# Last attention of an eight-sublayer network: the next layer's rows are normed by GpSimd, turned in other PSUM banks, and the router's products start inside the last unit

## The chip, the cores and the metric

The program runs on one core of one Trainium2 chip. The metric is the device time of one execution in microseconds (us), from the runs of the kernel. The core has five engines: TensorE (PE, matrix products and transposes, writes PSUM), VectorE (DVE), ScalarE (ACT), GpSimd (POOL, cannot read PSUM) and SyncE (SP, here the queue that issues the transfers). Each works through its own list of instructions in order and waits on semaphores for the others.

## The reference, cut to what matters

The network has four pairs of a cross-attention and a feed-forward part, each with a residual sum and a layer norm ahead of it. The change touches only the last pair. `x` is (8, 256, 512), the context (8, 256, 256).

```python
x = x + _L3_xattn_ref(_layernorm(x), ctx_1024, Wq, Wk, Wv, Wo, gq, gk)
x = x + _L3_ffn_ref(_layernorm(x), router_w, router_b, expert_w, expert_b)

def _layernorm(x, eps=1e-05):
    return (x - mean(x)) / sqrt(var(x) + eps)

def _L3_xattn_ref(h, c, Wq, Wk, Wv, Wo, gq, gk):       # 16 heads of 128
    q, k = rmsnorm(h @ Wq, gq), rmsnorm(c @ Wk, gk)    # per head
    attn = softmax(q k^T / sqrt(128))
    return (attn @ (c @ Wv)) @ Wo

def _L3_ffn_ref(x, router_w, router_b, expert_w, expert_b):   # 16 experts
    S = softmax(x.reshape(2048, 512) @ router_w + router_b)
    G, idx = top_k(S.T, 128)                                  # 128 tokens per expert
    ...                                                       # G * (tokens @ expert_w + expert_b), added back
```

## The kernel before

The residual stream `X` lies in SBUF as 16 tiles of 128 tokens by 512. A layer norm of tile t is: DVE takes the statistics (`dve_stat`: `st`, `mv`) and adds the epsilon (`sc`, L94); GpSimd raises it to -1/2 (`rsqrt`, L220, writes `rs`); DVE makes the normed rows `xn` (L95, two buffers, t mod 2); PE turns them with four 128x128 transposes into one PSUM bank (`pe_ln`, L218, banks 0 and 1 by t mod 2); ACT copies the bank to the high part `XH` (L84); DVE writes the low part `XL` = bank - `XH` (L90). Each product of the network is then three products of high and low parts.

The last attention is `wide_steps(3)`: 64 units, unit u for head pair u // 8 and batch u % 8, software-pipelined. All engines walk the same list of steps, and each issues its share of a step. The steps of unit u in order (letters of `order`):

- Q, `proj` u+1: PE makes the keys (bank 1), the queries (bank 0) and the values (bank 2). ACT squares the keys, DVE sums them (`kst`), GpSimd raises them (`kst`), DVE scales them to `K1` and writes `QL`, `VL`.
- 0, `out` (u-1, 0): PE multiplies the attention output by Wo (six products, bank 7), DVE adds the bank to the residual tile (`X<-X,banks`).
- T, `turn` u: PE turns the normalised probabilities `P` in banks 4 and 5, ACT and DVE split them into `PH`, `PL`.
- L, `late` u+1: PE turns `K1` in bank 1 and sums the squared queries with a column of ones; ACT and DVE write `KH`, `KL`; DVE writes `qst`, GpSimd raises it; `ctx` u+2: ACT and GpSimd split the context into `CH`, `CL`.
- 1, `out` (u-1, 1); S, `scores` u+1 (banks 2, 3; DVE maxima `mx`, `nb`; ACT exponentials `P`, L81); P, `pv` u (bank 6); N, `norm` u+1 (DVE `rc`, `P`); E, `pvout` u (`OH`, `OL`).

In the last eight units each `out` (v, i), v >= 56, completes a residual tile t = 2(v - 56) + i. Right behind it DVE takes the statistics of tile t and then does the whole norm step of tile t - 1 (`dve_ln`: `sc` of the next, `xn` of tile t, which waits for GpSimd's `rs`, and `XL` of tile t - 1); PE turns tile t - 1 right behind the `out` products (L827 and on), in bank 0 or 1, and so waits there:

```python
                if not l0 and (t := 2 * (v - 56) + i - 1) >= 0:
                    if v + 2 >= 64:
                        pe.wait_ge(S["kl3"], 64)
                        pe.wait_ge(S["qst"], 64)
                    elif t % 2:
                        pe.wait_ge(S["kst"], 3 * v + 9)
                    else:
                        pe.wait_ge(S["qst"], v + 3)
                    self.pe_ln(pe, 7, t)
```

Because bank 0 also holds the queries and bank 1 the keys, the following K turn and `proj` steps wait for `XL` of that tile (`wait_xt(pe, 7, ...)`). Behind the 64 units come three groups of router products (`pe_choice_logits` 0 to 2: 12 products of 16x512 each, banks 4 and 5), a fence of all engines, the turn of tile 15, router products 3, and 16 turns of the logits (`cWK`). From there the choice of tokens and the expert products run on; the change does not touch them.

Two steps `choice` (in units 58 and 59) put the split of the expert weights (`cwh` on ACT, `cwl` on DVE) behind those units.

Of the kernel before, what the change touches and what calls it, by code (L numbers as in the profile page):

```python
# [159 lines left out]
class Program:  # L160
# [184 lines left out]
    def act_ln(self, act, n, t):  # L345
# [10 lines left out]
        act.acopy((self.XH if n in LN_SPLIT else self.XF)[:, :, tok], src).then_inc(S["xh"], 1)  # L356

    def wait_xt(self, e, n, t):
# [8 lines left out]
    def wide_steps(self, L):  # L367
        l0 = L == 0

        if l0:  # L370
            yield "fetch", 0
            for t in range(4):
                yield "ln", t
            yield "part", 0
        yield "fetch", 1
        yield "proj", 0
        if not l0:
            yield "late", 0
            yield "ctx", 1
        yield "scores", 0  # L380
        yield "norm", 0
        side = 0
        for u in range(64):
            for step in "Q0TL1SPNE" if not l0 else "QT0SP1NE":
                if l0 and u >= 1 and step in "T0N" and side < NSIDE:
                    yield "side", side
                    side += 1
                if step == "Q" and u + 1 < 64:
                    if (u + 1) % 8 == 0:
                        yield "fetch", (u + 1) // 8 + 1  # L390
                    if (u + 1) % 8 == 5:
                        yield "part", (u + 1) // 8 + 1
                    yield "proj", u + 1
                    if not l0 and (u + 1) % 8 == 7:
                        yield "partkv", (u + 1) // 8 + 1
                if step == "T":
                    yield "turn", u
                if step == "L" and u + 1 < 64:
                    yield "late", u + 1
                    if u + 2 < 64:  # L400
                        yield "ctx", u + 2
                if step == "S" and u + 1 < 64:
                    yield "scores", u + 1
                if step == "0":
                    if u + 2 < NB:
                        yield "ln", 2 * u + 4
                        yield "ln", 2 * u + 5
                    if u >= 1:
                        yield "out", (u - 1, 0)
                if step == "1" and u >= 1:  # L410
                    yield "out", (u - 1, 1)
                if step == "P":
                    yield "pv", u
                if step == "E":
                    yield "pvout", u
                if step == "N" and u + 1 < 64:
                    yield "norm", u + 1
            if not l0 and u in (56, 58, 59):
                yield "choice", u
        yield "out", (63, 0)  # L420
        yield "out", (63, 1)

# [226 lines left out]
    def pool_wide(self, pool, L):  # L649
        S, w, l0 = self.S, self.W[L], L == 0  # L650
        n = 0 if l0 else 6
        for step, u in self.wide_steps(L):
# [11 lines left out]
            if not l0 and step == "late":  # L664
                pool.wait_ge(S["qst"], u + 1)
                pool.wait_ge(S["exp"], 4 * (64 + u))
                self.rsqrt(pool, w["qst"][:, 1, :], w["qst"][:, 0, :]).then_inc(S["qrs"], 1)
            if not l0 and step == "out" and (t := 2 * (u[0] - 56) + u[1] - 1) >= 0:
                self.pool_ln(pool, 7, t)

# [5 lines left out]
    def pe_wide(self, pe, L):  # L676
# [5 lines left out]
        for step, u in self.wide_steps(L):  # L682
# [11 lines left out]
            if step == "proj":  # L694
# [29 lines left out]
                if not l0:  # L724
                    pe.wait_ge(S["qst"], u)
                    if u >= 59:
                        self.wait_xt(pe, 7, 2 * u - 118)
                for h in range(2):
# [13 lines left out]
            if step == "late":  # L742
                k, z = banks[1], banks[0]
                pe.wait_ge(S["kst"], 3 * u + 3)
                if u < 7:
                    self.wait_xt(pe, n, min(2 * u + 3, NT - 1) if u else 3)
                if u >= 59:
                    self.wait_xt(pe, 7, 2 * u - 117)
                for i in range(2):
# [8 lines left out]
            if step == "turn":  # L758
                for qt in range(2):
                    z = banks[4 + qt]  # L760
                    pe.wait_ge(S["pl"], 2 * U - 1 + qt)
                    pe.wait_ge(S["n"], self.wide_n(L, u, 6))
                    for kt in range(2):
# [49 lines left out]
            if step == "out":  # L813
# [12 lines left out]
                pe.mms(z[:], terms).then_inc(S["y"], 1)  # L826
                if not l0 and (t := 2 * (v - 56) + i - 1) >= 0:  # L827
                    if v + 2 >= 64:
                        pe.wait_ge(S["kl3"], 64)
                        pe.wait_ge(S["qst"], 64)  # L830
                    elif t % 2:
                        pe.wait_ge(S["kst"], 3 * v + 9)
                    else:
                        pe.wait_ge(S["qst"], v + 3)
                    self.pe_ln(pe, 7, t)

    def act_wide(self, act, L):
# [9 lines left out]
        for step, u in self.wide_steps(L):  # L847
# [68 lines left out]
            if step == "out" and not l0 and (t := 2 * (u[0] - 56) + u[1] - 1) >= 0:  # L916
                self.act_ln(act, 7, t)

# [8 lines left out]
    def dve_wide(self, dve, L):  # L927
# [9 lines left out]
        for step, u in self.wide_steps(L):  # L937
# [11 lines left out]
            if step == "proj":  # L949
# [7 lines left out]
                else:  # L957
# [59 lines left out]
            if step == "out":  # L1017
# [2094 lines left out]
    def act_choice_logits(self, act, k):  # L3112
        S, w = self.S, self.W["c"]
        act.wait_ge(S["lz"], k + 5)
        act.acopy(w["WK"][:, 512 * k:512 * k + 512], self.banks[4 + k % 2][0:16, :]).then_inc(S["lg"], 1)

# [33 lines left out]
    def pe_choice(self, pe):  # L3150
        S, w, banks = self.S, self.W["c"], self.banks
        self.pe_ln(pe, 7, NT - 1)
        self.pe_choice_logits(pe, 3)
# [45 lines left out]
    def act_choice(self, act):  # L3199
        S, w, banks = self.S, self.W["c"], self.banks  # L3200
        self.act_ln(act, 7, NT - 1)
        self.act_choice_logits(act, 3)
# [24 lines left out]
    def dve_choice(self, dve):  # L3227
# [12 lines left out]

        self.dve_ln(dve, 7, NT - 1)
        dve.red(w["E16"][:], self.ident[:].rearrange("p (t e) -> p e t", t=8), ALU.add).then_inc(S["ctop"], 1)
# [106 lines left out]
    def pe_program(self, e):  # L3349
# [22 lines left out]
    def act_program(self, e):  # L3372
# [16 lines left out]
        self.act_wide(act, 3)  # L3389
        for k in range(3):  # L3390
            self.act_choice_logits(act, k)
        self.fence(act, 7)
# [142 lines left out]
```

## Time and profile before

| | us |
|---|---|
| median of 3 runs (3707.21 to 3717.07) | 3714.59 |
| the profiled execution, device time | 3713.18 |
| its span, first to last instruction | 3711.4 |
| PE busy | 3375.3 (91%) |
| DVE busy | 2365.6 (64%) |
| ACT busy | 1578.8 (43%) |
| POOL busy | 1255.7 (34%) |
| mean granted TensorE clock | 0.959 |

All positions below are microseconds from the start of the span. The last attention ends near 3640; the units before 3489 each take about 13.4 us. A busy share of a whole span is an average over unlike stages, so the stretch from 3462 to 3645 is read by itself: by windows that begin where DVE adds the first half of a unit's output to `X`, by DVE's waits, and by single rows of the timeline.

### The profile page before, as it was taken

The numbers are of one execution on the slowest core, as the hardware profiler recorded it, in microseconds if no ns is written. First come the engines' busy times: TensorE is split into PE (matmuls) and PEld (weight loads), VectorE is DVE, ScalarE is ACT, GpSimd is POOL, SyncE is SP. The second block draws the span as 40 slices with busy tenths as digits, with TensorE's granted clock in tenths as the row PEclk, the third lists the DMA queues.
The fourth block names the chain that finished last, engine by engine and source line by source line (L and its number), as shares of the span: only waits on it lengthen the run. The fifth ranks groups of instructions, "written<-read, shape, count | busy, mean of one in ns | idle before, by whom it ended". The sixth has DMA issues, their size and how long they took to land.

```text
span 3711.4 us, 60483 instructions
## 1 busy us (share of the span) xinstructions
PE 3375.3 (91%) x22678; PEld 2749.8 (74%) x22678; DVE 2365.6 (64%) x4653; ACT 1578.8 (43%) x3417; POOL 1255.7 (34%) x1168
## 2 busy tenths in 40 slices
PE   7999999959999689988999889997889999999977
PEld 6899998937778456656998644443789999999865
DVE  6677777863323478866444467774677777777766
ACT  5666665531111255542222233343245555555531
POOL 1013334111243477732222345554422222222212
PEclk9999999978999899999999889998999999999989
DMA  3246665124645110001111154542000000000001
GB/s 131 80 135 224 231 224 181 37 86 164 242 172 191 69 28 28 11 5 69 35 35 38 30 139 113 128 116 50 27 7 18 13 18 18 18 7 18 13 1 48
DMA packets 153784, 296.92 MB, mean 80 GB/s; under 512 B 18040, under 2 KB 71416, under 8 KB 148760
## 3 DMA queue, kind: packets, MB, share of 16 engines
q1 hardware_dynamic: 147256, 272.60, 23.1%
q0 software_dynamic: 6240, 20.45, 1.6%
q8 instruction: 184, 3.01, 0.3%
q14 instruction: 104, 0.85, 0.1%
HBM read 390.12 MB, written 95.68 MB: 131 GB/s over the span
## 4 chain that ended last, share of the span: by engine, by line
PE 37%; DVE 8%; issue 3%; POOL 2%; ACT 1%; DMA 1%; SPq 0%; POOLq 0%; DVEq 0%; ACTq 0%
PE banks L107 34%; PE banks L218 3%; DVE nrec L2656 1%; DVE nmx L101 1%; ACT P L81 1%; DVE xn L95 0%; POOL kst L90 0%; DVE X L90 0%; DMA nqT<-nmT 0%; DVE st L274 0%; DVE PL L90 0%; DVE X L98 0%; POOL rs L90 0%; DVE KL L98 0%; DVE P L94 0%
## 5 line engine op out<-in xcount | busy, mean ns | idle before, releaser
L90 DVE TENSOR_TENSOR X<-X,banks 128x512 f32<-128x512 f32 x352 | 239.9, 683 | 192.5 <-PE banks L107 192.2
L101 DVE TENSOR_REDUCE nmx<-banks 128x4 f32<-128x1024 f32 (+2 forms) x256 | 238.8, 954 | 122.3 <-PE banks L107 122.2
L81 ACT ACTIVATE nPT<-banks 128x1024 f32<-128x1024 f32 x192 | 196.4, 1023 | 239.8 <-PE banks L107 239.6
L107 PE MATMUL banks<-XH,wqh 128*128 128x256 f32 x1024 | 292.3, 285 | 0.0
L107 PE MATMUL banks<-XL,wqh 128*128 128x256 f32 x1024 | 286.7, 280 | 0.0
L107 PE MATMUL banks<-XH,wql 128*128 128x256 f32 x1024 | 286.4, 280 | 0.0
L107 PE MATMUL banks<-XH,tT 128*128 128x256 f32 x1024 | 246.3, 284 | 8.3 <-DVE XL L90 5.4
L90 POOL TENSOR_TENSOR slo<-sraw,shi 128x512 fp32r<-128x512 f32 x96 | 126.0, 1313 | 374.7 <-ACT shi L84 374.7
L107 PE MATMUL banks<-XL,tT 128*128 128x256 f32 x1024 | 245.1, 283 | 0.0
L107 PE MATMUL banks<-woh,OH 128*128 128x512 f32 x512 | 219.3, 428 | 12.2 <-DVE OL L90 10.3
L81 ACT ACTIVATE P<-banks,nb,qst 128x256 f32<-128x256 f32 x256 | 141.2, 561 | 190.7 <-DVE nb L90 190.7
L107 PE MATMUL banks<-WU,exh 128*128 (+1 forms) x624 | 207.5, 404 | 14.3 <-DMA WU<-expert_parts 12.7
L107 PE MATMUL banks<-woh,OL 128*128 128x512 f32 x512 | 206.6, 404 | 0.0
L107 PE MATMUL banks<-wol,OH 128*128 128x512 f32 x512 | 206.5, 403 | 0.0
L107 PEld LDWEIGHTS banks<-XH,tT 128*128 128x128 f32 x1024 | 196.7, 192 | 11.1 <-DVE XL L90 7.1
L90 POOL TENSOR_TENSOR nPS<-nPT 128x512 f32<-128x512 f32 x128 | 162.6, 1271 | 114.7 <-PE banks L107 95.9
L107 PEld LDWEIGHTS banks<-XL,tT 128*128 128x128 f32 x1024 | 196.7, 192 | 0.8
L107 PEld LDWEIGHTS banks<-XH,wqh 128*128 128x128 f32 x1024 | 195.8, 191 | 0.0
L107 PEld LDWEIGHTS banks<-XL,wqh 128*128 128x128 f32 x1024 | 193.8, 189 | 0.0
L107 PEld LDWEIGHTS banks<-XH,wql 128*128 128x128 f32 x1024 | 193.5, 189 | 0.0
L90 POOL TENSOR_TENSOR kst<-kst,mhalf 128x4 f32<-128x4 f32 x64 | 64.6, 1009 | 364.7 <-DVE kst L95 364.7
L90 DVE TENSOR_TENSOR PL<-banks,PH 128x512 fp32r<-128x512 f32 x256 | 164.6, 684 | 29.9 <-ACT PH L84 29.0
(443 smaller groups left out, 10122.6 us busy)
## 6 DMA issues: line engine op xcount, KB each, us to landing
WU<-expert_parts SPq DMA_DIRECT2D x39, 4096.0 KB
WD<-expert_parts SPq DMA_DIRECT2D x39, 2048.0 KB
sraw<-in_moe_w SPq DMA_DIRECT2D x96, 256.0 KB, 3.3
expert_parts<-shi SPq DMA_DIRECT2D x96, 256.0 KB
expert_parts<-slo SPq DMA_DIRECT2D x96, 256.0 KB
head_stacks<-nTK SPq DMA_DIRECT2D x48, 256.0 KB
head_stacks<-nTQ SPq DMA_DIRECT2D x48, 256.0 KB, 3.0
nkT<-head_stacks SPq DMA_DIRECT2D x64, 192.0 KB, 4.5
```

What stands on the lines that cost most here:

```text
L81: return self.e.activation(out, in_, func, **kw)
L90: return self.e.tensor_tensor(out, a, b, op)
L101: return self.e.tensor_reduce(out, a, AX.X, op, **kw)
L107: return self.e.matmul(out, l, r, start=start, stop=stop, skip_group_check=skip)
L218: return pe.e.transpose(out, in_, self.ident[0:n, 0:n])
L2656: dve.e.reciprocal(w["rec"][:], z[:, 256:512]).then_inc(S["n_r"], 1)
```

## The change

`LATE = {3: 7}`: in attention 3 the rows of norm 7 take a new path, the `late_*` functions. DVE keeps the statistics, `sc` and `XL`. GpSimd makes `rs` and now also `xn` (`pool_late`). PE turns in banks 4 and 5 (the probabilities') at a new step M at the end of a unit: tile 0 in unit 57, then two tiles per unit (1, 2 in unit 58, up to 11, 12 in unit 63), 13 and 14 behind the last two `out` steps, 15 behind the fence. `XL` of two tiles is written by DVE in the next unit between `kst` and `K1`. The waits of the `proj` and `late` steps for `XL` go; the turn of the probabilities gets one. In unit 63 the order is `aT0PE1Mb`: router products 0 ahead of the last turn of probabilities, router products 1 behind the turns of tiles 11 and 12, products 2 behind tile 14; they use banks 0 and 1.

```diff
+    def late_tiles(self, u):
+        return [t for t in (2 * u - 115, 2 * u - 114) if t >= 0] if u >= 57 else []
+    def dve_late_stat(self, dve, n, t):
+        self.dve_stat(dve, n, t)
+        self.dve_ln_var(dve, n, t)
+    def pool_late(self, pool, n, t):
+        S = self.S
+        pool.wait_ge(S["var"], ln_var(n, t))
+        self.rsqrt(pool, self.rs[:, t:t + 1], self.sc1[:, t:t + 1]).then_inc(S["rs"], 1)
+        pool.wait_ge(S["ln_turned"], ln_at(n, t - 2))
+        pool.wait_ge(S["rs"], ln_rs(n, t))
+        pool.ts(self.xn[:, t % 2, :], self.X[:, t, :], self.mv[:, t, 0:1], self.rs[:, t:t + 1], ALU.subtract, ALU.mult
+                ).then_inc(S["xn"], 1)
+    def pe_late(self, pe, n, t, U0):
+        S, z = self.S, self.banks[4 + t % 2]
+        pe.wait_ge(S["pl"], 2 * (U0 + min(57 + (t + 1) // 2, 63)) + 2)
+        if t >= 2:
+            pe.wait_ge(S["xl"], ln_xl(n, t - 2))
+        pe.wait_ge(S["xn"], ln_at(n, t))
...
+    def act_late(self, act, n, t):
...
+    def dve_late_low(self, dve, n, t):
...
@@ wide_steps
-            for step in "Q0TL1SPNE" if not l0 else "QT0SP1NE":
+            order = "QT0SP1NE" if l0 else "Q0TL1SPNE"
+            if L in self.LATE:
+                order = "aT0PE1Mb" if u == 63 else order + "M"
+            for step in order:
...
+                if step == "M":
+                    for t in self.late_tiles(u):
+                        yield "late_ln", t
+                if step in "ab":
+                    yield "logits", "ab".index(step)
...
-        yield "out", (63, 0)
-        yield "out", (63, 1)
+        for i in range(2):
+            yield "out", (63, i)
+            if L in self.LATE:
+                yield "late_ln", 13 + i
+        if L in self.LATE:
+            yield "logits", 2
@@ pool_wide
-            if not l0 and step == "out" and (t := 2 * (u[0] - 56) + u[1] - 1) >= 0:
-                self.pool_ln(pool, 7, t)
+            if L in self.LATE and step == "out" and u[0] >= 56:
+                t = 2 * (u[0] - 56) + u[1]
+                if l0 or u[0] >= 62:
+                    self.pool_late(pool, self.LATE[L], t)
+                elif u[1]:
+                    for i in (t - 1, t):
+                        self.pool_late(pool, self.LATE[L], i)
@@ pe_wide (proj, then late)
-                    if u >= 59:
-                        self.wait_xt(pe, 7, 2 * u - 118)
-                if u >= 59:
-                    self.wait_xt(pe, 7, 2 * u - 117)
@@ pe_wide (turn)
+                    for t in self.late_tiles(u - 1) if L in self.LATE else []:
+                        self.wait_xt(pe, self.LATE[L], t)
@@ dve_wide (proj, between kst and K1)
+                    for t in self.late_tiles(u - 2):
+                        self.dve_late_low(dve, 7, t)
@@ dve_wide (out)
-                    self.dve_stat(dve, 1 if l0 else 7, t)
-                    if not l0 and t:
-                        self.dve_ln(dve, 7, t - 1)
+                    if L in self.LATE:
+                        self.dve_late_stat(dve, self.LATE[L], t)
...
+            if step == "late_ln" and (l0 or u >= 9):
+                self.dve_late_low(dve, self.LATE[L], u)
@@ pe_choice_logits
-        z, tok = self.banks[4 + k % 2], slice(512 * k, 512 * k + 512)
+        z, tok = self.banks[k % 2], slice(512 * k, 512 * k + 512)
...
-            pe.wait_ge(S["pl"], 2 * 128)
+            pe.wait_ge(S["ql"], 128)
+            pe.wait_ge(S["qst"], 64)
+            pe.wait_ge(S["kl3"], 64)
@@ pe_program, act_program
-        for k in range(3):
-            self.pe_choice_logits(pe, k)
```

How the lists move is shown at two places. First VectorE, behind unit 58, before (names are the tiles written and read; `K_206` is `K1`):

```order
L101 TENSOR_REDUCE kst_256<-banks 128x4
L95 TENSOR_SCALAR kst_256<-kst_256 128x4
L90 TENSOR_TENSOR K_206_254<-banks,kst_256 128x512
L90 TENSOR_TENSOR QL_227<-banks,QH_226 128x512
L90 TENSOR_TENSOR VL_231<-banks,VH_230 128x512
L90 TENSOR_TENSOR X_49<-X_49,banks 128x512
L274 BN_STATS st_58<-X_49 128x6
L276 BN_AGGR mv_56<-st_58 128x2
L94 TENSOR_SCALAR sc_12_60<-mv_56 128x1
L95 TENSOR_SCALAR xn_59<-X_49,mv_56,rs_57 128x512
L90 TENSOR_TENSOR XL_51<-banks,XH_50 128x4x128
L90 TENSOR_TENSOR PL_234<-banks,PH_233 128x512 x2
```

and now:

```order
L101 TENSOR_REDUCE kst_256<-banks 128x4
L95 TENSOR_SCALAR kst_256<-kst_256 128x4
L90 TENSOR_TENSOR XL_51<-banks,XH_50 128x4x128 x2
L90 TENSOR_TENSOR K_206_254<-banks,kst_256 128x512
L90 TENSOR_TENSOR QL_227<-banks,QH_226 128x512
L90 TENSOR_TENSOR VL_231<-banks,VH_230 128x512
L90 TENSOR_TENSOR X_49<-X_49,banks 128x512
L274 BN_STATS st_58<-X_49 128x6
L276 BN_AGGR mv_56<-st_58 128x2
L94 TENSOR_SCALAR sc_12_60<-mv_56 128x1
L90 TENSOR_TENSOR PL_234<-banks,PH_233 128x512 x2
```

`xn` is gone from behind `sc`, and both `XL` stand between `kst` and `K1`; a second `xn` and `XL` behind the other `X` of the unit are gone too. Second GpSimd, one unit of the last eight, before:

```order
L90 TENSOR_TENSOR kst_256<-kst_256,mhalf_55 128x4
L90 TENSOR_TENSOR rs_57<-sc_12_60,mhalf_55 128x1
L90 TENSOR_TENSOR qst_257<-qst_257,mhalf_55 128x4
L90 TENSOR_TENSOR CL_243<-CTX_52,CH_242 128x512
L90 TENSOR_TENSOR rs_57<-sc_12_60,mhalf_55 128x1
```

and now:

```order
L90 TENSOR_TENSOR kst_256<-kst_256,mhalf_55 128x4
L90 TENSOR_TENSOR qst_257<-qst_257,mhalf_55 128x4
L90 TENSOR_TENSOR CL_243<-CTX_52,CH_242 128x512
L90 TENSOR_TENSOR rs_57<-sc_12_60,mhalf_55 128x1
L95 TENSOR_SCALAR xn_59<-X_49,mv_56,rs_57 128x512
L90 TENSOR_TENSOR rs_57<-sc_12_60,mhalf_55 128x1
L95 TENSOR_SCALAR xn_59<-X_49,mv_56,rs_57 128x512
```

Both `rs` of a unit now stand behind `qst` and `CL`, and each is followed by its `xn`.

## Rows read from the trace of the kernel before

**Rows 1.** Windows: start:end, us, busy us (count) per engine, PEclk, DMA share, GB/s
```profile
3475.68:3489.12 13.44, 13.44 (x106) 12.87 (x105) 9.72 (x22) 7.15 (x17) 3.27 (x3) 1.00 0.00 1
...
3573.69:3594.32 20.63, 16.35 (x115) 14.83 (x114) 13.74 (x32) 8.32 (x20) 4.37 (x5) 0.92 0.00 1
3594.32:3645.15 50.83, 34.76 (x163) 23.45 (x162) 25.39 (x57) 12.42 (x26) 5.83 (x15) 0.87 0.02 6
```

**Rows 2.** Waits of PE, 3489.2 to 3645.1: total us, times, longest
```profile
PE banks L218 <- DVE XL L90: 15.5, 5, 3.3
```

**Rows 3.** Waits of DVE in one late unit, 3573.7 to 3594.3
```profile
DVE X L90 <- PE banks L107: 2.0, 1, 2.0
DVE rc L1000 <- ACT P L81: 1.6, 1, 1.6
DVE xn L95 <- POOL rs L90: 1.5, 2, 0.7
DVE K L90 <- POOL kst L90: 1.2, 1, 1.2
```

**Rows 4.** Timeline of PE in undisturbed units: start, us, instruction
```profile
3464.04 0.48 PE L107 MATMUL banks<-woh,OH 128*128 128x512 f32 x1
3465.51 0.28 PE L107 MATMUL banks<-KH,QH 128*128 128x256 f32 x1
3468.38 0.28 PE L107 MATMUL banks<-kvh,CH 128*128 128x256 f32 x1
3475.37 1.03 PE L218 MATMUL banks<-ident,P 128*128 128x128 f32 x8
3476.24 0.60 PE L218 MATMUL banks<-ident,K 128*128 128x128 f32 x4
```

**Rows 5.** Timeline of DVE in the same undisturbed units
```profile
3464.39 0.74 DVE L98 SCALAR_TENSOR_TENSOR KL<-banks,gqk,KH 128x512 fp32r<-128x512 f32 x1
3465.71 0.69 DVE L90 TENSOR_TENSOR X<-X,banks 128x512 f32<-128x512 f32 x1 [0.51 <-PE banks L107]
3471.20 0.68 DVE L90 TENSOR_TENSOR OL<-banks,OH 128x512 fp32r<-128x512 f32 x1
3476.64 1.29 DVE L90 TENSOR_TENSOR PL<-banks,PH 128x512 fp32r<-128x512 f32 x2 [0.28 <-ACT PH L84]
```

**Rows 6.** Timeline of GpSimd: its row powers and context split, undisturbed unit
```profile
3465.28 1.01 POOL L90 TENSOR_TENSOR qst<-qst,mhalf 128x4 f32<-128x4 f32 x1 [4.97 <-DVE qst L94]
3466.26 1.29 POOL L90 TENSOR_TENSOR CL<-CTX,CH 128x512 fp32r<-128x512 f32 x1
```

**Rows 7.** Timeline of DVE in a late unit: residual sum to low probabilities
```profile
3594.32 0.68 DVE L90 TENSOR_TENSOR X<-X,banks 128x512 f32<-128x512 f32 x1
3596.86 0.55 DVE L95 TENSOR_SCALAR xn<-X,mv,rs 128x512 f32<-128x512 f32 x1 [0.73 <-POOL rs L90]
3597.32 0.68 DVE L90 TENSOR_TENSOR XL<-banks,XH 128x512 fp32r<-128x512 f32 x1
3597.92 1.28 DVE L90 TENSOR_TENSOR PL<-banks,PH 128x512 fp32r<-128x512 f32 x2
```

**Rows 8.** Timeline of GpSimd in a late unit: the row power of one tile
```profile
3583.60 0.55 POOL L90 TENSOR_TENSOR rs<-sc,mhalf 128x1 f32<-128x1 f32 x1 [1.60 <-DVE sc L94]
```

**Rows 9.** Groups by line, whole span: GpSimd's copy of 128x512 (mean 639 ns)
```profile
L87 POOL COPY slo<-sraw 128x512 f32<-128x512 f32 x4 | 2.6, 639 | 6.2 <-DMA expert_parts<-slo 3.3 <-DMA sraw<-in_L_ffn_factors 2.9
```

**Rows 10.** Tile `nb`, 2700 to 3480: durations ns, least/median/longest
```profile
L90 DVE TENSOR_TENSOR nb<-mx,qst x110: 160/282/582, 2713.3 to 3468.2; 128x2 f32<-128x2 f32 x110
```

**Rows 11.** Timeline of ACT and DVE behind unit 59: the split of expert weights
```profile
3545.34 1.07 ACT L84 ACTIVATE cwh<-craw 128x1024 fp32r<-128x1024 f32 x1
3546.88 1.21 DVE L90 TENSOR_TENSOR cwl<-craw,cwh 128x1024 fp32r<-128x1024 f32 x1
```

**Rows 12.** Timeline of PE behind the fence: turn of tile 15, turns of the logits
```profile
3639.36 0.66 PE L218 MATMUL banks<-ident,xn 128*128 128x128 f32 x4 [0.71 <-ACTq L213]
3645.15 1.16 PE L218 MATMUL banks<-ident,cWK 16*128 16x16 f32 x16 [0.68 <-ACT cWK L84]
```

More of the change, by code:

```diff
@@ L356, in act_ln @@
         act.acopy((self.XH if n in LN_SPLIT else self.XF)[:, :, tok], src).then_inc(S["xh"], 1)
+    LATE = {3: 7}
+    def late_tiles(self, u):
[17 more added lines that the diff above has]
+        pe.wait_ge(S["xn"], ln_at(n, t))
+        for k in range(4):
+            m = self.turn(pe, z[:, 128 * k:128 * k + 128], self.xn[:, t % 2, 128 * k:128 * k + 128])
+        m.then_inc(S["ln_turned"], 1)
+    def act_late(self, act, n, t):
+        S, tok = self.S, slice(128 * t, 128 * t + 128)
+        act.wait_ge(S["ln_turned"], ln_at(n, t))
+        act.acopy(self.XH[:, :, tok], self.banks[4 + t % 2][:].rearrange("p (c n) -> p c n", c=4)).then_inc(S["xh"], 1)
+    def dve_late_low(self, dve, n, t):
+        S, tok = self.S, slice(128 * t, 128 * t + 128)
+        dve.wait_ge(S["xh"], ln_at(n, t))
+        dve.tt(self.XL[:, :, tok], self.banks[4 + t % 2][:].rearrange("p (c n) -> p c n", c=4), self.XH[:, :, tok].bitcast(F32),
+               ALU.subtract).then_inc(S["xl"], 1)
     def wait_xt(self, e, n, t):
@@ L826, in pe_wide @@
                 pe.mms(z[:], terms).then_inc(S["y"], 1)
[L827 to L835, printed above, removed]
+            if step == "late_ln":
+                self.pe_late(pe, self.LATE[L], u, U0)
+            if step == "logits":
+                self.pe_choice_logits(pe, u)
     def act_wide(self, act, L):
@@ L915, in act_wide @@
                 act.acopy(w["OH"][:], banks[6][:].rearrange("p (h n) -> p h n", h=2)).then_inc(S["oh"], 1)
-            if step == "out" and not l0 and (t := 2 * (u[0] - 56) + u[1] - 1) >= 0:
-                self.act_ln(act, 7, t)
+            if step == "late_ln":
+                self.act_late(act, self.LATE[L], u)
+            if step == "logits":
+                self.act_choice_logits(act, u)
     def dve_mask(self, dve):
@@ L1024, in dve_wide @@
                     dve.wait_ge(S["xadd"], 2 * U + i + 1)
-                    self.dve_stat(dve, 1 if l0 else 7, t)
-                    if not l0 and t:
-                        self.dve_ln(dve, 7, t - 1)
+                    if L in self.LATE:
+                        self.dve_late_stat(dve, self.LATE[L], t)
+                    else:
+                        self.dve_stat(dve, 1, t)
+            if step == "late_ln" and (l0 or u >= 9):
+                self.dve_late_low(dve, self.LATE[L], u)
     def route_steps(self):
@@ L3114, in act_choice_logits @@
         act.wait_ge(S["lz"], k + 5)
-        act.acopy(w["WK"][:, 512 * k:512 * k + 512], self.banks[4 + k % 2][0:16, :]).then_inc(S["lg"], 1)
+        act.acopy(w["WK"][:, 512 * k:512 * k + 512], self.banks[k % 2][0:16, :]).then_inc(S["lg"], 1)
     def sp_choice(self, sp):
@@ L3151, in pe_choice @@
         S, w, banks = self.S, self.W["c"], self.banks
-        self.pe_ln(pe, 7, NT - 1)
+        self.pe_late(pe, 7, NT - 1, 64)
         self.pe_choice_logits(pe, 3)
@@ L3200, in act_choice @@
         S, w, banks = self.S, self.W["c"], self.banks
-        self.act_ln(act, 7, NT - 1)
+        self.act_late(act, 7, NT - 1)
         self.act_choice_logits(act, 3)
@@ L3239, in after @@
             dve.wait_ge(S["ctop"], k)
-        self.dve_ln(dve, 7, NT - 1)
+        self.dve_late_low(dve, 7, NT - 1)
         dve.red(w["E16"][:], self.ident[:].rearrange("p (t e) -> p e t", t=8), ALU.add).then_inc(S["ctop"], 1)
@@ L3389, in act_program @@
         self.act_wide(act, 3)
-        for k in range(3):
-            self.act_choice_logits(act, k)
         self.fence(act, 7)
```

## The prediction

> **What bounds the kernel now.** Only the last eight units of the last attention and the stretch up to the logits' turns change, so I cut the trace there, by windows that begin where DVE adds `out` (v, 0) to `X` [rows 1]. The unit ahead, 3475.68 to 3489.12, takes 13.44 us with PE busy for all of it at full clock: PE bounds an undisturbed unit. The five units behind it, up to 3594.32, take 105.2 us together, the last of them 20.63 with PE busy for 16.35 and DVE for 13.74: neither is full, so a chain through several engines is the bound. The waits say which: PE waits 15.5 us in five places for `XL` of the norm before it may turn `K1` [rows 2]. In one such unit DVE waits 2.0 us for PE's output products, 1.6 for the exponentials, 1.5 for GpSimd's `rs` (twice) and 1.2 for `kst` [rows 3]. So the norm step of every half unit lies in series: product, `X`, statistics, `rs`, `xn`, `XL`, and then the K turn. PE's granted clock is 0.92 in that unit and 0.87 in the tail, against 1.00 before [rows 1]; it falls behind the long waits. From 3594.32 to the turns of the logits at 3645.15 come another 50.83 us, where PE works for 34.76.
>
> **What the change does to a unit.** I work out the three loops that could set its length.
>
> PE: 13.44 us plus two turns of four transposes. The eight transposes of `P` begin at 3475.37 and K's at 3476.24, so four cost 0.43 [rows 4]. PE's loop is 13.44 + 0.87 = 14.3 us.
>
> DVE: the late unit of 20.63 us less its waits of 6.3 is 14.3 [rows 1, 3]. Two `xn` go; one occupies the engine from 3596.86 to 3597.32, 0.46 us [rows 7], so 13.4 are left. The wait of 1.6 for the exponentials stays: 15.0. The 1.2 us wait for `kst` is filled by the two `XL`, which take 0.60 each (3597.32 to 3597.92) [rows 7]; they were in the 13.4 already. The waits for `rs` fall away with `xn`. If the two `nb` are held up now and then as today (median 0.28, least 0.16) [rows 10], DVE's loop is about 15.3.
>
> The chain through all: the second turn at M (tile 2u - 114) needs the `xn` that GpSimd can make only behind `qst` and `CL` of the same unit, and it now stands ahead of the next `proj`. From `X` to `PL`: 3594.32 to the start of `xn`, less its 0.73 of waiting, is 1.81. `PL` 1.20. `KL` to GpSimd's `qst` 0.89 (3464.39 to 3465.28) [rows 5, 6]. `qst` 0.98, `CL` 1.29 [rows 6], `rs` 0.60 [rows 8], `xn` on GpSimd x, a hand-over of 0.07 (my allowance), the turn 0.43. Then keys, queries, values and output products to the next turn of `P`, 6.99 (3468.38 to 3475.37); the output group is 1.47 of this (3464.04 to 3465.51), and it is 1.67 from its start to DVE's `X` (3464.04 to 3465.71) [rows 4, 5], so 6.99 - 1.47 + 1.67 = 7.19. The sum is 14.46 + x.
>
> x is not in the trace: a GpSimd operation of 128x512 with one tensor input and two scalars per row. The copy of 128x512 takes 0.64, the subtraction of two such tensors 1.29 [rows 9, 6]. It has one input like the copy and arithmetic like the other; I take 0.9, nearer to the copy. The loop is 15.4 us. In the Trainium skill, GPSIMD Engine Reference, section 3.1, a one-input loop over 512 elements takes 769 ns at best; by that the loop would be 0.13 us shorter. The copy's 0.64 is below that figure, so the row does not bear it out as a floor.
>
> So a plain late unit is set by this chain, 15.4 us, with DVE at 15.3 close behind. The first of the five starts with GpSimd idle and one tile to turn: 15.2. Behind units 58 and 59 ACT's `cwh` (1.07) stands between `XH` and the square of the keys, and DVE's `cwl` (1.21) follows it [rows 11]; without them the square (0.6) would stand there. That adds 1.6 to 1.7 to DVE's loop, 16.7. The five units: 15.2 + 2 x 16.7 + 2 x 15.4 = 79.4 against 105.2. **Gain 25.8.**
>
> **The tail**, counted from `X` (61, 0) at zero (3594.32 before). `X` to `PL` 1.81, `PL` to `X` (61, 1) about 2.0, so 3.8; from there an undisturbed unit has 5.49 to `OL` (3465.71 to 3471.20) [rows 5], plus 1.1 of statistics (1.81 less the 0.71 of `X`): 10.4. `XL` 9 and 10 end at 12.3, and the turn of `P` waits for them. Turn to `PL` is 1.27 (3475.37 to 3476.64) [rows 4, 5], `PL` 1.2: 14.8. `pv` 1.44 (half of scores and `pv`, 3465.51 to 3468.38) [rows 4], output products (62, 1) 1.47: 17.7. Tile 11 is turned at once; tile 12 waits for its `xn` (`X` 14.85, statistics to 16.65, `rs`, `xn` to 18.4), done at 18.85. Router products 1, twelve at 0.23 (six take 1.4 to 1.47 [rows 4]), 2.8: 21.65. Output (63, 0) to `X` 1.67, statistics 1.8, `rs` and `xn` of tile 14 1.85, turn 0.43, router products 2 2.8: 30.2. ACT's copy and the fence 0.75: 30.95. Then turn of tile 15 to logits' turns as today, 5.79 (3639.36 to 3645.15) [rows 12]: 36.7 against 50.83. **Gain 14.1.** Router products 0 cost nothing: they fill PE while it waits for `XL` 9 and 10. If that cover went, they would cost 2.8. Behind the logits' turns nothing changes.
>
> The sum is 39.9. From it I take 4 us for the clock: behind units 58 and 59 PE still idles 16.7 - 14.3 = 2.4 us, and a unit of today at 0.92 loses 0.08 x 20.63 = 1.65 us of clock; two of these and 0.7 in the tail. Net 36. The sum is made against the profiled execution, 3713.2 (span 3711.4), which is 1.4 below the median of the three runs, well inside their scatter of 10. **3713.2 - 36 = 3677 us.**
>
> What is late next: GpSimd's `xn` at the second turn and `KL` ahead of the scores, together 1.1 us of PE's waiting in a plain unit (15.4 - 14.3). Queued behind the waiting turn on PE is the whole next `proj`; behind GpSimd's wait for the turn of tile t - 2 is only the next `kst`, due some 3 us later. SP's queue is not passed by anything.
>
> **Rivals.**
> 1. *No chain closes, PE is the bound.* For it: the chain exceeds PE's loop by only 1.1. Then three units of 14.3, no clock loss and x at 0.64: 3.3 + 4 + up to 2 less, **3668**. Chance 0.10.
> 2. *GpSimd and DVE hold each other.* `nb` has two SBUF inputs and takes between 0.16 and 0.58 us [rows 10]: its longer cases say it waits for something, and GpSimd's `CL` runs beside it (3466.26 to 3467.55). With `rs` and `xn` now beside both `nb`, each could wait out an `xn`, 0.9 or 1.3: DVE's loop is 15.0 + 1.8 to 2.6, so five units cost 1.5 to 2.2 more each, 8 to 11 in all: **3686**. Chance 0.12. This is the rule in the Trainium skill, SBUF — State Buffer, section "Who interferes with whom": the port pair shared by DVE and GpSimd is an exclusive lock, and a DVE instruction with two SBUF inputs contends with a GpSimd one that reads SBUF. The longer `nb` of today agree with it. By the same rule most of DVE's work here, with one input from PSUM, stays free of it, which is why I keep this below the forecast.
> 3. *The clock keeps falling.* Each late unit now still has waits ahead of a turn, and as today each loses 1.65 to 3.3 us (0.92 to about 0.85): 5 x 2.5 less the 4 counted, and 3 in the tail: 11 more, **3688**. Chance 0.17.
> 4. *Slower: PE stays at 1.2 GHz through the late units.* All PE work of a unit, 14.3 us, lies on the chain or close to it. At half rate it is up to 28 us a unit, 140 against 105.2; the tail's PE part, some 20 of 36.7, doubles too, 57 against 50.8: 41 more, **3754**. It decides from an average unit of 23.9 us on ((105.2 + 14.1) / 5), which needs a mean clock near 0.6; today's, with more idling, is 0.85 to 0.92. Chance 0.02.
> 5. *The change does not shorten what sets the end*, for instance GpSimd's `xn` takes 5 us because of two per-row scalars: the chain is 19.5, five units 97.5, a gain of 7.7; the tail's two `xn` add 8 and leave 6.1 of its gain; less the 4 for the clock 10 are left, **3703**. Chance 0.04.
>
> **The numbers.** The forecast has 0.55. Its own range is the sum with x between 0.64 and 1.29 (five places on the path, -1.3 to +2), the clock term between 0 and 8, and 2 us of small hand-overs: 3671 to 3684. With rivals 1 to 3 the range for 8 in 10 is 3666 to 3692. A measurement of this kernel can tell about 0.3% (11 us) from no change. Faster by more than that: all but rivals 4 and 5, 0.94; within it 0.04; slower 0.02.
>
> **What would show it.** In windows from `X` to `X`: five units of 15 to 17 us where 19 to 22 stood, the last unit's DVE waits for `rs` gone and no wait of PE for `XL` ahead of the K turn. PE waits below 1 us for GpSimd's `xn` at the second turn. GpSimd's `xn` near 0.9 us. `X` (61, 0) to the logits' turns near 37. A PEclk column above 0.95. Wrong, if GpSimd's `xn` takes over 2 us, if PE waits 2 us or more for `xn`, if `nb` lasts about 1 us, or if the clock column stays below 0.9.

## The result, and the profile after

| | before | after |
|---|---|---|
| median of the runs shown side by side, us | 3713.32 (4 runs, 3707.21 to 3717.07) | 3677.90 (4 runs, 3674.84 to 3687.26) |
| profiled execution, device time | 3713.18 | 3674.84 |
| its span | 3711.4 | 3673.0 |
| X (56, 0) to X (61, 0), five units | 105.20 | 82.98 |
| X (61, 0) to the logits' turns, the tail | 50.83 | 38.85 |

The ratio of the times is 0.991, 95% interval 0.9895 to 0.9925. So the time fell by 0.9%, clear of the scatter. The forecast was 3677. Two windows of the trace after, the third late unit and the tail, in the columns of [rows 1]:

```profile
3517.08:3533.67 16.59, 14.78 (x114) 13.66 (x113) 13.87 (x30) 9.17 (x20) 8.80 (x7) 1.00 0.01 2
3566.86:3605.71 38.85, 30.63 (x170) 19.81 (x168) 22.27 (x50) 12.34 (x26) 18.37 (x21) 1.00 0.03 8
```

All five units take 16.6 us, whether the split of the expert weights stands behind them or not, and the clock is 1.00 in every one and in the tail, where the windows of before had 0.91, 0.92, 0.85, 0.84 and 0.92, and 0.87 in the tail [rows 1]. Busy GpSimd rises from 4.37 to 8.80 us in a unit. What PE waits for now, 3480 to 3640 (total us, times, longest), against the 15.5 us for `XL` of [rows 2]:

```profile
PE banks L218 <- POOL xn L95: 12.1, 8, 2.5
PE banks L218 <- DVE XL L90: 0.8, 1, 0.8
```

One late unit on DVE, GpSimd and PE (timeline: start, us, instruction, idle time before it and what ended it). DVE first, then GpSimd, then PE's turns of the two tiles:

```profile
3518.82 1.28 DVE L90 TENSOR_TENSOR PL<-banks,PH 128x512 fp32r<-128x512 f32 x2
3520.01 0.74 DVE L98 SCALAR_TENSOR_TENSOR KL<-banks,gqk,KH 128x512 fp32r<-128x512 f32 x1
3533.67 0.69 DVE L90 TENSOR_TENSOR X<-X,banks 128x512 f32<-128x512 f32 x1
```
```profile
3520.90 1.01 POOL L90 TENSOR_TENSOR qst<-qst,mhalf 128x4 f32<-128x4 f32 x1 [5.93 <-DVE qst L94]
3521.88 1.30 POOL L90 TENSOR_TENSOR CL<-CTX,CH 128x512 fp32r<-128x512 f32 x1
3523.13 0.56 POOL L90 TENSOR_TENSOR rs<-sc,mhalf 128x1 f32<-128x1 f32 x1
3523.86 2.08 POOL L95 TENSOR_SCALAR xn<-X,mv,rs 128x512 f32<-128x512 f32 x1 [0.18 <-POOL rs L90]
```
```profile
3523.85 0.60 PE L218 MATMUL banks<-ident,xn 128*128 128x128 f32 x4
3525.99 0.66 PE L218 MATMUL banks<-ident,xn 128*128 128x128 f32 x4 [1.55 <-POOL xn L95]
```

The chain of the prediction, from start to start: X at 3517.08, `PL` 1.74 later, `KL` 1.19, `qst` 0.89, `CL` 0.98, `rs` 1.25, `xn` 0.73, the second turn 2.13, and 7.68 from there to the next X at 3533.67, together 16.59. From `PL` to the turn each row starts as the one before it ends, or within 0.2 us of it; that this chain sets the unit is what e1 and e2 test. The first turn of the pair, the tile of the unit before, waits for nothing.

From profile to profile the span fell by 38.4 us: 22.22 in the five units, 11.98 in the tail, 5.24 because this execution came to X (56, 0) at 3483.88 where that of before came at 3489.12, less 1.04 behind the logits. What the change did is the 34.2 us of the first two; e11 is about the 5.24. A good part of the 34.2 may be the clock: the granted clocks of before, weighed with their windows, come to 11.9 us in the five units and 6.6 in the tail, and nothing is lost after. These 18.5 us are an estimate from above, since a low clock costs nothing while PE waits. No run parts the shorter chain from the clock that came back with it.

### The profile page after: what moved, and what is told of

It is laid out like the page before. It is cut to its first block, busy times and chain, and to the rows that moved or that the text cites. A ratio compares the mean times of both kernels' runs of the same rounds, so it can differ in the third digit from the quotient of the medians.

```text
span 3673.0 us, 60478 instructions
## 1 busy us (share of the span) xinstructions
PE 3358.4 (91%) x22678; PEld 2736.7 (75%) x22678; DVE 2352.1 (64%) x4637; ACT 1578.6 (43%) x3417; POOL 1292.3 (35%) x1184
## 4 chain that ended last, share of the span: by engine, by line
PE 37%; DVE 7%; issue 3%; POOL 2%; ACT 1%; DMA 1%; SPq 0%; POOLq 0%; DVEq 0%; ACTq 0%
PE banks L107 34%; PE banks L218 3%; DVE nrec L2715 1%; DVE nmx L101 1%; DVE PL L90 1%; DVE X L90 1%; POOL CL L90 0%; DMA nqT<-nmT 0%; DVE st L274 0%; DVE X L98 0%; DVE KL L98 0%; POOL xn L95 0%; POOL qst L90 0%; POOL kst L90 0%; DVE xn L95 0%
## 5 line engine op out<-in xcount | busy, mean ns | idle before, releaser
L107 PE MATMUL banks<-WU,exh 128*128 (+1 forms) x624 | 206.3, 402 | 11.6 <-DMA WU<-expert_parts 10.1
```

The source lines that it names most:

```text
L107: return self.e.matmul(out, l, r, start=start, stop=stop, skip_group_check=skip)
```

## The experiments

Effects of 3 to 12 us are 0.1 to 0.3% of the time, no more than the scatter of a few executions. So each verdict goes by windows cut at the same instructions, five units and tail as in the table above. An edit is shown against the changed kernel, if nothing else is said.

**e1, GpSimd makes each xn at its own step**

```diff
-                if l0 or u[0] >= 62:
-                    self.pool_late(pool, self.LATE[L], t)
-                elif u[1]:
-                    for i in (t - 1, t):
-                        self.pool_late(pool, self.LATE[L], i)
+                self.pool_late(pool, self.LATE[L], t)
```

> Edit: GpSimd makes `rs` and `xn` of each tile at that tile's own `out` step, so the first tile's pair comes ahead of `qst` and `CL` instead of behind them; everything else as in the changed kernel. Theory (the chain X, PL, KL, qst, CL, rs, xn, turns, X sets the 16.6 us of a late unit, with `xn` at 2.08 us): `xn` of a unit's first tile leaves the chain, PE's and DVE's own loops are next, at 14.4 and 14.7 us (16.2 where cwl is added): units 57, 60 and 61 about 14.7, 58 and 59 about 16.2, five units 76.6 instead of 83.0, so -6.4 us; the tail hardly moves (38.9, down to 38.5). Rival A (the engines are full, or GpSimd's longer work slows DVE): the five units stay at 82 to 83, -1 us at most. Rival B (the later qst holds DVE's `nb`): `nb` over 0.2 us and units between 15.5 and 16.6.

Measured: units 15.15, 16.95, 16.80, 15.19 and 15.20, five units 79.29 (-3.7), tail 39.17; median 3677.64 of 4 runs (3676.16 to 3680.20), not to be told from the changed kernel's; this trace had come to X (56, 0) 6.1 us later than the one above. The first turn no longer waits and the unit falls as far as another loop allows. That loop is DVE's, and half a microsecond longer than the theory said. DVE's timeline and GpSimd's in the fifth unit say why:

```profile
3560.18 0.88 DVE L90 TENSOR_TENSOR nb<-mx,qst 128x2 f32<-128x2 f32 x1
```
```profile
3559.75 1.30 POOL L90 TENSOR_TENSOR CL<-CTX,CH 128x512 fp32r<-128x512 f32 x1
```

`nb` works on 2 columns and takes 0.16 us when nothing holds it; here it takes 0.88 and ends at 3561.06, when `CL` ends (3561.05). The first `nb` of an undisturbed unit does the same in the kernel before: 0.42 us from 3467.15, where `CL` ends at 3467.55 [rows 6]. So the long `nb` of rival B is there, held by `CL` and not by the later `qst` as it had it (in e5, with `CL` moved ahead, `nb` is short again). It is rival 2 of the prediction, real in this kernel though not in the late units of the changed one.

**e2, every late xn made twice**

```diff
+        pool.ts(self.xn[...], self.X[:, t, :], ...).then_inc(S["xtwice"], 1)
+        pool.wait_ge(S["xtwice"], t + 1)
         pool.ts(self.xn[...], self.X[:, t, :], ...).then_inc(S["xn"], 1)
```

> Edit: GpSimd makes every late `xn` twice, the second behind the first, and only the second is waited for by the turns. Theory (GpSimd's xn is on the chain of every late unit): one more `xn` of 2.08 us and a semaphore of some 0.1 to 0.2 us per tile; the chain from one X to the next holds one `xn`, so a unit grows from 16.6 to about 18.8, five units from 83.0 to 94, and the tail, whose gaps at xn 12 and xn 14 lie open, by 4 to 6: +15 to +17 us. Rival (GpSimd is off the path and PE or DVE sets the unit): within 1 us of 83.0 and 38.9.

Measured: units of 20.5, five units 102.5 (+19.5), tail 49.4 (+10.6), one time of 3706.32. One `xn` more is on the chain, as expected, but it adds 3.9 us to a unit instead of 2.2. The rest is the clock. PE in the third unit:

```profile
3537.47 1.12 PE L218 MATMUL banks<-ident,xn 128*128 128x128 f32 x4 [3.93 <-POOL xn L95]
...
3538.60 0.41 PE L107 MATMUL banks<-kvh,CL 128*128 128x256 f32 x1
...
3540.71 0.27 PE L107 MATMUL banks<-kvl,CH 128*128 128x256 f32 x1
```

Behind 3.93 us of idling the products take 0.41 us where they take 0.28 at full clock; the window's granted clock is 0.92. From the turn to the first query product is 3.35 us (3537.47 to 3540.82) against 1.93 in the changed kernel (3525.99 to 3527.92): 1.4 us of clock per unit, and 2.4 of `xn` (4.46 less 2.08).

**e3, what xn costs in four forms**

```diff
+        if t % 4 == 1:
+            i = pool.ts(o, x, 0.0, 1.0, ALU.subtract, ALU.mult)
+        if t % 4 == 2:
+            i = pool.ts(o, x, r, None, ALU.mult)
+        if t % 4 == 3:
+            i = pool.ts(o, x, 1.0, None, ALU.mult)
```

> Edit: the late `xn` is made in four forms by tile number mod 4: (0) as it is, two operations with two scalars per row; (1) two operations with constants 0.0 and 1.0; (2) one operation with one scalar per row; (3) one operation with the constant 1.0. Forms 1 to 3 leave out the norm or a part of it, and the output changes with it. This measures the price of `xn` alone: the forecast took 0.9 us from the copy's 0.64 and the two-input operation's 1.29, and the trace shows 2.08. Theory A (the scalars read per row are what costs): form 1 about as quick as form 3, near 0.7 to 1.0, form 2 about 1.3 to 1.5. Theory B (each operation is a pass of its own): forms 0 and 1 both near 2.1, forms 2 and 3 near 1.0 to 1.3.

The tile's groups (ns least/median/longest, first and last start):

```profile
L95 POOL TENSOR_SCALAR xn<-X,mv,rs x4: 2080/2082/2083, 3494.6 to 3587.5; 128x512 f32<-128x512 f32 x4
L95 POOL TENSOR_SCALAR xn<-X x4: 1931/2119/2121, 3497.5 to 3592.3; 128x512 f32<-128x512 f32 x4
L94 POOL TENSOR_SCALAR xn<-X,rs x4: 1577/1577/1581, 3511.2 to 3597.1; 128x512 f32<-128x512 f32 x4
L94 POOL TENSOR_SCALAR xn<-X x4: 1495/1557/1621, 3513.5 to 3599.6; 128x512 f32<-128x512 f32 x4
```

Theory B: the scalars per row cost nothing, the second arithmetic operation costs 0.5 us. But one operation takes 1.56 to 1.58, over the 1.0 to 1.3 that it allowed, and far over the copy's 0.64 [rows 9]. The copy was the wrong neighbour: a TENSOR_SCALAR with one input costs more than a TENSOR_TENSOR with two (1.30). The unit of tiles 6 and 7, both with the short forms, takes 16.08 instead of 16.59: the 0.5 us taken off `xn` show up in full. In that of tiles 2 and 3 they do not (16.51): there DVE runs without a gap from its wait for the exponentials to the next X, with `crl` and `cwl` behind `OL` and P<-P,rc at 1.85 instead of 1.14 beside the one-operation form. The tail took 39.92, with 7.19 us from the turn of tile 15 to the logits' turns at a clock of 0.76, where the changed kernel has 5.82 at 1.00.

**e4, the split of the expert weights behind units 62 and 63**

```diff
-            if not l0 and u in (56, 58, 59):
+            if not l0 and u in (56, 58, 62, 63):
```

> Edit: `cwh` and `cwl` (the split of the expert weights, 1.07 us on ACT and 1.21 us on DVE) move from behind units 58 and 59 to behind units 62 and 63. Theory (the chain through GpSimd leaves DVE idle for longer than cwl takes, so both lie hidden in the changed kernel): units 58 and 59 stay at 16.6, the five units at 83.0, 0 us; in the tail at most +1. Rival (cwl was on the path, as the forecast had it with 16.7 against 15.4): units 58 and 59 drop by 1.2 each, -2.5 us.

Measured: units 16.58 to 16.60, five units 82.96, so `cwl` lay hidden in the changed kernel: its DVE loop of 14.7 + 1.5 stays under the chain's 16.6. In the tail the theory's "+1 at most" fails: 41.72 instead of 38.85. The first split adds 1.30 (X (62, 0) to X (63, 0): 10.94 against 9.64), and 1.57 are clock (X (63, 0) to the turn of tile 15: 10.54 against 8.97 at a granted clock of 0.84).

**e5, CL ahead of qst and xn on GpSimd**, against e1, with `powers` for the `qst` operation, followed by the held `xn`:

```diff
                 self.pool_ctx(pool, u)
+                if held is not None:
+                    powers(u - 1)
```

> Edit: as e1, with GpSimd's list of a late unit in another order: `rs` of the first tile at its own step, then `CL`, `qst`, `xn` of the first tile, `rs` and `xn` of the second (e1: rs, xn, qst, CL, rs, xn). What is asked: e1's units took 15.2 us where its theory said 14.7, and in each of them DVE's first `nb` took 0.88 us instead of 0.16 and ended when `CL` ended. Theory (GpSimd's two-input CL holds the small DVE operation until it is done, and this lies on the path to the exponentials): with CL moved ahead, nb is back at 0.16 and units 57, 60, 61 take 14.5 to 14.7, units 58 and 59 16.1 to 16.3; five units 76 to 77 against 79.3 in e1 and 83.0 in the changed kernel; P<-P,rc may grow from 1.15 to 1.5 under the second xn (as in e2), which would give back up to 0.35 per unit. Rival (the 0.7 was something else, or DVE's loop is simply longer than I count): units stay at 15.2 and 16.9, five units 79.

Measured: units 14.75, 16.23, 16.08, 14.81 and 14.82, five units 76.69, `nb` at 0.16 to 0.19 again and P<-P,rc at 1.49. The theory holds, with the plain units 0.1 us over its range. The tail took 42.28 instead of 38.85: 0.35 in its first window, 1.58 behind the wait for tile 14 (clock 0.84) and 1.51 behind the fence (clock 0.77). PE behind its wait for `xn` of tile 14:

```profile
3592.89 0.63 PE L218 MATMUL banks<-ident,xn 128*128 128x128 f32 x4 [2.46 <-POOL xn L95]
...
3593.58 0.40 PE L107 MATMUL banks<-XL,crh 128*16 128x512 f32 x1
...
3594.21 0.63 PE L107 MATMUL banks<-XH,crh 128*16 128x512 f32 x1
```

The products go from 0.40 to 0.63 us shortly behind a wait of 2.46; in the changed kernel they stay at 0.40 behind one of 2.48.

**e6, VectorE makes every late xn**

```diff
+                if L in self.LATE and 58 <= u <= 63:      # norm, ahead of rc
+                    self.dve_ln_norm(dve, 7, 2 * (u - 58))
+                if L in self.LATE and 57 <= u <= 62:      # behind OL
+                    self.dve_ln_norm(dve, 7, 2 * (u - 57) + 1)
```

> Edit: VectorE makes all late `xn` again (0.55 us each): the first of a unit while it waits for the exponentials, the second behind `OL`, those of tiles 12 to 15 right behind their statistics; GpSimd makes only `rs`, at each tile's own step. The new banks, the new place of the turns and of XL and the router products stay. Theory (what paid in the change is the new place of turns and XL; the move of xn to GpSimd did not, at 2.08 us on the chain it even costs): units 57, 60, 61 at 15.2 to 15.5, units 58 and 59 at 16.4 to 16.8, five units 78.5 to 80 against 83.0; the tail 36.2 against 38.9. Rival (GpSimd had to take xn, VectorE is too full for it): a late unit of 17 us or more, five units 86 and above.

Measured: units 15.25, 16.22, 16.05, 15.26 and 15.27, five units 78.05 (-4.9, a little better than the theory), tail 37.09 (-1.8, where it had -2.7), one time of 3672.88. So VectorE's `xn` beats GpSimd's as the change places it. It does not beat GpSimd's in the late units as e5 places it: there they take 76.69. In those units the order of GpSimd's list was what cost, not the engine; in the tail VectorE is the quicker one.

**e7, router products behind the last unit**

```diff
-                order = "aT0PE1Mb" if u == 63 else order + "M"
+                order = "T0PE1M" if u == 63 else order + "M"
...
-            yield "logits", 2
+            for k in range(3):
+                yield "logits", k
```

> Edit: router products 0, 1 and 2 all stand behind the last unit again (still in banks 0 and 1), instead of 0 ahead of the last turn of probabilities, 1 behind the turns of tiles 11 and 12, 2 behind tile 14. Theory: the 12 products of a group (2.8 us on PE) ran where PE would have waited for XL and for `OL`; put at the end they lie open: products 0 +2.8, products 1 about +1.0, tail 38.9 -> 42.7, five units unchanged at 83.0. Rival (PE is full in the tail, the products only change places): tail within 0.5 of 38.9.

Measured: five units 82.95, tail 44.91, +6.1 instead of +3.8. Without products 0, PE waits 3.60 us for `XL` 9 and 10 instead of 0.81, and its clock is 0.80 in the window of 16.46 us that had taken 14.42 at 1.00. So in this trace products 0 do more than fill a gap: with the gap open the clock came down, at a price of 2.0 us. The clock fell once more behind a wait of 2.40 for tile 14 (0.92 over the last 21.18 us, some 1.7 us by estimate), as it did in e4 and e5 with the products in place. That part cannot be put down to the edit, and the products' own work then lies open for some 2.3 us, not 3.8.

**e8, e5 and xn of tiles 12 to 15 on VectorE**

```diff
         self.dve_ln_var(dve, n, t)
+        if t >= 12:
+            self.dve_ln_norm(dve, n, t)
```

> Edit: e5, and VectorE makes `xn` of tiles 12 to 15 right behind their statistics (GpSimd only their `rs`). Theory: the late units as in e5 (76 to 77 for five); in the tail PE's waits for xn of tile 12 (1.11 us) and of tile 14 (2.48 us) shrink, tail 38.9 -> 36.4; together 9 to 10 us less than the changed kernel, about 3669 where that is at 3678. Rival: what is saved in the late units comes back in the tail or in the later start of something else, and the time stays within 3 us of the changed kernel's.

Measured: 3666.57 median of 4 runs (3661.26 to 3667.53), ratio to before 0.9869, interval 0.9852 to 0.9885, wholly under the changed kernel's (0.9895 to 0.9925): the five units 76.68, the tail 37.06 (36.4 expected), by windows 8.1 us less than the changed kernel where 9 to 10 were expected. The wait for `xn` of tile 14 is 0.85, and the one for tile 12 is gone.

**e9, on the kernel before: GpSimd makes xn, nothing else**

```diff
                 self.rsqrt(pool, self.rs[:, k:k + 1], self.sc1[:, k:k + 1]).then_inc(S["rs"], 1)
+                if n == 7:
...
+                    pool.ts(self.xn[:, k % 2, :], self.X[:, k, :], ...).then_inc(S["xn"], 1)
```

> Edit, on the kernel before: GpSimd makes `xn` of norm 7 right behind each `rs`, VectorE no longer makes it; nothing else of the change (turns in banks 0 and 1 right behind the `out` products, router products behind the last unit, XL of tile t-1 right behind the statistics of tile t). What is asked: which part of the change paid. Theory A (XL is what PE waits for, and before it VectorE waits for rs, 0.7 us, and makes xn, 0.55 us; taken away, XL comes up to 1.28 us earlier per tile): the late units of before, 19.2 to 22.2 us, shorten by 1.3 to 2.6 each, total -8 to -15, and PE's wait for XL of 15.5 us falls. Theory B (GpSimd's xn of 2.08 us stands ahead of qst and the kst power, which nb and K wait for, and gives it back): within 4 us of the kernel before, with new waits of DVE on GpSimd.

Measured: 3700.35 median of 7 runs, ratio 0.9960, interval 0.9949 to 0.9972. Five units 95.14 (-10.1; the first takes 21.83 where before had 19.18, the four others 18.0 to 18.9), tail 47.68 (-3.2), PE's wait for `XL` 8.3 us instead of 15.5. Theory A holds for the sum; of B a part shows, the waits for GpSimd now in PE's list:

```profile
PE banks L218 <- POOL xn L95: 8.7, 3, 5.3
PE banks L218 <- DVE XL L90: 8.3, 5, 2.0
```

So the move alone was worth 13 us in the old order, where VectorE's wait for `rs` and its `xn` stood ahead of `XL`; two of its five units run at clock 1.00, so part of this too can be the clock. In the new order, where `XL` waits for neither, the order of the change on GpSimd, with `CL` and `rs` between `qst` and `xn`, takes the gain back (e5, e6).

**e10, e8 with the split in ACT's and DVE's idle places**

```diff
                     yield "out", (u - 1, 0)
+                    if not l0 and u == 63:
+                        yield "choice", 62
...
+                if i:
+                    yield "choice", 63
@@ dve_choice, behind the fence
+        self.dve_choice_early(dve, 1)
         self.dve_late_low(dve, 7, NT - 1)
```

> Edit: e8, with the split of the expert weights moved from behind units 58 and 59 to places where ACT and DVE are idle: `cwh` and `cwl` of the first half behind `out` (62, 0) in unit 63 (ACT idle 4.36, DVE 1.10 us there in e8), `cwh` of the second half behind the turn of tile 14 and its `cwl` behind the fence ahead of XL of tile 15 (DVE idle 1.55). Theory: units 58 and 59 fall from 16.2 and 16.1 to 14.8 each, five units from 76.7 to 73.9; the tail grows by 0.1 to 1.0: -2 to -2.8 us against e8, about 3664. Rival (as in e4, what moves to the tail lies open there: e4's tail was 41.7 instead of 38.9, part of it clock): tail +2 to +3, no gain over e8.

Measured: units 14.74 to 14.88, five units 74.06 as expected. The tail took 38.49, though up to the fence it is 0.08 quicker than in e8 (31.16 from X (61, 0) to the turn of tile 15, against 31.24). Behind the fence the trace of e10, and then that of e8:

```profile
3592.18:3599.51 7.33, 5.18 (x17) 1.91 (x17) 2.38 (x4) 1.18 (x2) 2.34 (x8) 0.77 0.14 38
```
```profile
3592.35:3598.17 5.82, 3.60 (x16) 1.47 (x17) 1.16 (x3) 1.18 (x2) 1.50 (x8) 1.00 0.20 48
```

The same instructions of PE take 1.5 us longer at a clock of 0.77. That DVE's `cwl` stands there now is not needed for it: e5 took 7.33 us for this stretch at 0.77 and e3 7.19 at 0.76, both without `cwl` in it. The median is 3668.53 of 5 runs (3668.03 to 3675.85), ratio 0.9884, interval 0.9868 to 0.9901: 2.6 us won in the units, no gain over e8 to be measured.

**e11, the changed kernel once more**

> The changed kernel itself once more, unedited, for a second trace. What is asked: whether the 5.2 us by which its profile entered the late units earlier than that of before belongs to the change, and whether the clock stays full behind the 2.48 us wait of PE for xn of tile 14. Theory (both are differences between executions): X of unit 56 anywhere between 3484 and 3490, the five units again 83.0 within 0.1; the tail 38.9, or 41 to 42 where the clock falls behind that wait, as it did in e4 and e5. Rival (the early entry is the change's): again 3484 within 0.5.

Measured: 3677.80. X (56, 0) at 3487.82, five units 82.99, tail 38.86 at clock 1.00, behind a wait of 2.47 for tile 14. So the units and the tail repeat to 0.01 us, and most of the early entry was that execution's: over the eleven traces with the changed schedule X (56, 0) comes between 3483.9 and 3490.0, 3487.3 on average, with the same instructions ahead of it. The two traces with the old schedule have 3489.12 and 3492.16 (e9), too few to rule out a small part for the change. With this trace the difference to before is 35.4 us of span, all but 1.2 of it in the five units and the tail.

## Why the prediction was right

The mechanism was right: a chain through GpSimd sets a plain late unit, and its terms other than GpSimd's `xn` are right to 0.05 us in sum. That the time (3677 forecast, 3677.9 measured) came out within 1 us is luck: a term too small by 1.2 us on every plain unit and a loss of 4 us that did not come cancel for the most part. By its own steps:

- **The bound before and the three loops.** Right in kind. A plain late unit is set by the chain through GpSimd that was written down: 14.46 + x, with x at the measured 2.08, gives 16.54, and the trace has 16.59. The loops behind it were near: DVE's was put at 15.3 and turned out at 14.8 (e5), PE's at 14.3, which no run reached.
- **x, GpSimd's `xn`, taken as 0.9 with bounds 0.64 and 1.29.** This term was mis-sized: it measures 2.08, outside both bounds. The nearest rows were chosen by the number of inputs; e3 shows that the kind of operation decides. It cost 1.2 us in each plain unit, 1.4 in the first, and is the likely cause of the 2.2 in the tail (38.85 measured, 36.7 forecast), where two `xn` stand on the path. By the prediction's last part this alone, `xn` over 2 us and waits of PE for it of 2.01 (first unit) and 2.48 (tile 14), was a sign of being wrong; it was wrong in that term.
- **16.7 us behind units 58 and 59.** Right by accident: 16.59 is the chain. The split adds 1.3 to 1.75 us to DVE's loop, near the 1.6 to 1.7 of the forecast (e1, e5; gone in e10), but lies under a longer chain (e4).
- **The first late unit, 15.2.** It is 16.61; the chain closes there with one tile already.
- **4 us for the clock.** It did not come: 1.00 in the late units. PE's waits of 1.55 (2.01 in the first unit) left the clock alone, and 2.4 us behind the split, on which the term rested, never arose. Five units and tail gained 34.2 us where 39.9 were summed and, less 4 for the clock, 36 forecast: 5.7 lost, mostly on x, and 4 given back by a loss that did not come.
- **Router products 0 cost nothing.** Right, and short of the truth: in e7's trace the gap that they fill brought the clock down, 2.0 us on top of the work that lies open at the end.
- **Rival 1, PE is the bound:** no unit fell under 14.7 in any run. **Rival 2, GpSimd and DVE hold each other:** not in the changed kernel, where all ten `nb` of the five units take 0.160 to 0.162 us, because they fall behind `CL`, beside `rs` and `xn`; it is real where `CL` meets `nb` (e1). The exclusive lock that the prediction took from the Trainium skill, SBUF — State Buffer, section "Who interferes with whom", agrees with e1's `nb` and `CL` (both with two SBUF inputs). Against it stands that no `xn`, which reads SBUF as well, held `nb` to its end: beside the two-operation form it took 0.16 in the changed kernel (at 3523.98, `xn` from 3523.86) and in e5 (at 3493.03, `xn` from 3491.80 to 3493.88), and 0.34 to 0.35 in e9 (at 3522.50, `xn` from 3522.06 to 3524.14). **Rival 3, the clock keeps falling:** it needed longer waits; e2 is what it would have looked like. **Rival 4, PE stays at 1.2 GHz:** the clock was 1.00. **Rival 5, xn at 5 us:** its mechanism, at two fifths of its size.

Which part of the change paid: not one by itself. GpSimd's `xn` alone gives 13 of the 34 us (e9); everything else with `xn` on VectorE gives 41 (105.20 + 50.83 less 78.05 + 37.09 in e6), and with `xn` on the engine that did better in each part, on GpSimd for the units and on VectorE for the tail, 42 (e8). Both take the wait for `rs` and the `xn` away from in front of `XL`, so they share that gain. That the new banks by themselves, or the new place of `XL` by itself, gives a certain part of the rest was not tried.

## What to carry to other kernels

A step that is moved to an idle engine goes into a chain as well as off one: add up the chain from an instruction to its own next round, and run the operation once on its new engine before counting on it, since kinds of operation cost differently there and a copy says little of arithmetic. When a new order has taken the work off the path, ask again where it belongs: here another order of the same engine's list gave 6.3 us in the late units (e5), and the old engine 1.8 in the tail (e8). Filling a gap ahead of a TensorE step can be worth more than the work put there, where the gap would bring the clock down (e7, one trace).

## What the hardware showed

- GpSimd, 128x512 in f32: TENSOR_SCALAR with two operations 2.08 us (up to 2.27 for the second of a unit, why is open), with one 1.56 to 1.58 in the median, scalars per row or constants alike (e3); TENSOR_TENSOR 1.30; COPY 0.64 [rows 9].
- A DVE operation of 2 columns with two SBUF inputs lasted until GpSimd's two-input CL was done (0.88 us instead of 0.16), each time they met (e1, 0.87 to 0.92 in five units). P<-P,rc (SBUF to SBUF) took 1.49 to 1.54 instead of 1.14 beside the two-operation `xn` and 1.85 beside the one-operation form (e3); the Trainium skill, SBUF — State Buffer, section "Who interferes with whom", counts DVE's tensor_scalar among the operations that can take the shared ports. These rows agree that GpSimd hinders it, but P<-P,rc only ran longer and did not wait for the end of the `xn`. Operations of DVE that read PSUM kept their 0.68 beside either.
- TensorE's granted clock fell behind waits of 3.93 and 3.60 us (e2, e7) and stayed full behind 1.55 and 2.01, in the units of every trace that had them. Behind the wait of 2.40 to 2.48 for tile 14 it stayed in three traces (the changed kernel twice, e1) and fell in four (e4, e5, e7, e9), at a price of 1.6 to 1.7 us. Behind the fence it fell in three (e3, e5, e10: 7.19 to 7.33 us at 0.76 to 0.77) and stayed in all the others (5.8 us at 1.00). What separates these cases the runs do not show. A difference of 1.5 to 3 us in a single trace of this kernel can be this alone.
